# Attention of a six-stage decoder block on one core: row-tiled scores, column-tiled values, reciprocals folded into the turning matmuls

## The reference

```python
q, k, v = (x @ Wq.T), (x @ Wk.T), (x @ Wv.T)        # each (8, 256, 16, 32)
scores = einsum('bqhd,bkhd->bhqk', q, k) / sqrt(32)
scores = where(causal_mask, scores, finfo.min)
attn = einsum('bhqk,bkhd->bqhd', softmax(scores), v)
x = layernorm(x + attn.reshape(8, 256, 512) @ Wo.T)
```

## Time and profile before

| | us |
|---|---|
| median of 3 runs | 3803.29 |
| the profiled execution's own time | 3801.35 |
| its span | 3799.4 |
| attention, first matmul to last addition | 23.1 to 529.4 |
| layer norm after it begins | 531.1 |

### The profile page before, as it was taken

One profiled execution on the slowest core, in us unless ns is written; L12 is line 12 of the kernel. 1 busy time (PEld: TensorE's weight loads), 2 busy tenths in 40 slices (PEclk: granted clock), 3 DMA queues, 4 the chain that ended last, 5 costly groups with the idle time before them and its releaser, 6 DMA issues. The chain is left out here.

```text
span 3799.4 us, 82582 instructions
## 1 busy us (share of the span) xinstructions
PE 3343.9 (88%) x29419; PEld 2405.9 (63%) x29438; DVE 2678.5 (70%) x4880; ACT 2129.4 (56%) x5227; POOL 1348.2 (35%) x1657
## 2 busy tenths in 40 slices
PE   7999978724799999999999999999999999994285
PEld 6788855523567677677776676767776767672142
DVE  3445449977477777777777777777777777776896
ACT  2233330023577777777776767767777677763453
POOL 0000014401345454545454454545454545440000
PEclk9999989967899999999999999999999999996698
DMA  2000011100110101001101010001010100001201
GB/s 106 13 7 12 12 74 41 36 19 19 42 35 20 33 18 41 30 24 29 41 18 36 18 40 29 24 30 40 18 35 19 41 29 24 29 18 45 89 1 45
DMA packets 44277, 121.73 MB, mean 32 GB/s; under 512 B 5856, under 2 KB 11104, under 8 KB 40544
## 3 DMA queue, kind: packets, MB, share of 16 engines
q1 hardware_dynamic: 43872, 116.35, 9.5%
HBM read 111.80 MB, written 4.54 MB: 31 GB/s over the span
## 5 line engine op out<-in xcount | busy, mean ns | idle before, releaser
L1885 DVE TENSOR_TENSOR delta_Pb<-delta_bank,delta_lev 128x512 f16<-128x512 f32 x448 | 311.9, 696 | 228.4 <-PE delta_bank L2198 228.4
L1877 DVE SCALAR_TENSOR_TENSOR delta_F<-delta_bank,delta_cw,delta_F 128x510 f32<-128x510 f32 (+1 forms) x512 | 381.8, 746 | 94.1 <-ACT delta_far L1695 82.6
L1491 POOL TENSOR_TENSOR delta_F<-delta_F,delta_far 128x506 f32<-128x506 f32 x256 | 282.6, 1104 | 435.7 <-DVE delta_F L1877 434.8
L2172 PE MATMUL delta_bank<-delta_xh,delta_qkvh 128*128 128x512 f16 x1024 | 389.8, 381 | 5.4 <-DVE delta_qkvl L1845 3.0
L2172 PE MATMUL delta_bank<-delta_xl,delta_qkvh 128*128 128x512 f16 x1024 | 390.1, 381 | 0.0
L2172 PE MATMUL delta_bank<-delta_xh,delta_qkvl 128*128 128x512 f16 x1024 | 389.6, 380 | 0.0
L1689 ACT ACTIVATE delta_F<-delta_bank,delta_cw 128x512 f32<-128x512 f32 x256 | 178.3, 697 | 313.4 <-PE delta_bank L2172 312.2
L1894 DVE CAST delta_XT<-delta_bank 128x512 f16<-128x512 f32 x448 | 309.5, 691 | 45.5 <-PE delta_bank L2221 45.3
L1471 POOL TENSOR_SCALAR_AFFINE_SELECT delta_LA<-delta_LA 128x512 f32<-128x512 f32 x128 | 81.3, 635 | 651.6 <-DVE delta_LA L1905 649.9
L2157 PE MATMUL delta_bank<-delta_zh,delta_xh 128*128 128x256 f16 x1024 | 280.2, 274 | 0.6 <-ACT delta_gz L1717 0.6
L2157 PE MATMUL delta_bank<-delta_zl,delta_xh 128*128 128x256 f16 x1024 | 279.9, 273 | 0.0
(11 more groups left out here) (311 smaller groups left out, 9776.9 us busy)
## 6 DMA issues: line engine op xcount, KB each, us to landing
delta_Gb<-g_rows SPq DMA_DIRECT2D x66, 512.0 KB, 5.2
delta_st_qkv<-in_Wqkv SPq DMA_DIRECT2D x17, 1024.0 KB, 8.2
conv_T<-filters SPq DMA_DIRECT2D x32, 256.0 KB, 3.1
delta_st_zo<-in_Wz SPq DMA_DIRECT2D x16, 512.0 KB, 8.4
delta_st_zo<-in_Wout SPq DMA_DIRECT2D x16, 512.0 KB, 6.2
ffn_ahead_W<-in_W SPq DMA_DIRECT2D x2, 4096.0 KB, 17.2
conv_ahead_C<-in_ctx_rev SPq DMA_DIRECT2D x1, 6144.0 KB, 17.3
attn_xt<-in_xT SPq DMA_DIRECT2D x10, 512.0 KB, 4.0
```

What stands on the lines that cost most here:

```text
L1491: gp.tensor_tensor(dst[:, :, 3:256], dst[:, :, 3:256], src[:, :, 0:253], ALU.add)\
L1877: ve.scalar_tensor_tensor(dst, src, cw_tap(i, 3 - lag), dst, ALU.mult, ALU.add)\
L1885: ve.tensor_tensor(left(Pb[:, lvl, :, :], lvl), comp(bank[5], lvl), bc(lev[:, lvl, :].rearrange("p (n s) -> p n s", s=1 << lvl), 1, 8), AL ...
L2172: ins = te.matmul(bk[:, :], ww[:, QKV[job], kc, :], xx[:, kc, tok:tok + 512], start=(m == 0), stop=(m == 11))
```

## The change

The hardware loop is gone: `attn_uses` writes out the order, for `GROUPS` = 32 jobs. A job is one batch's four heads that share a 128-feature tile, both query halves together.

- q is no longer padded. It is copied like k, by ScalarE, in one instruction of 128 partitions (`Q2`). A head's scores are a matmul on its own 32 partitions (`Q[32 * r:32 * r + 32, ...]`), with r = 0 to 3 in four banks of `sc4`. The mask comes first: one bf16 matmul of 384 columns a head, then 256 columns of scores for the second queries, then 128 for the first. `sc4` has one copy: the scores of job j wait for the exponentials of job j-1.
- `transposes` become `turn`: each 128x128 block of exponentials is the stationary operand of an ordinary float32 matmul with `dg`, a diagonal matrix of the reciprocal row sums. GpSimd makes the eight diagonals of a job in one instruction of 1024 elements a partition. `normalise` and the transposes L300 go.
- `values` has v's 32 columns as stationary operand and the turned probabilities as moving one (256 columns, then 128), and writes partitions 32r to 32r+31 of `vb`: the output is made transposed, as the Wo product needs it; ScalarE copies it (`acopy`).
- All projections and Wo products share one bank, `ub`. Up to three of these uses stand in each slot of a job: the first ahead of the turns, the second ahead of the third turn, the third ahead of the values.
- Each weight matrix has its own semaphore; q0, k0, v0, v1 of batch 0 come first. Eight batches are projected, none for nothing. The second slice of x is loaded ahead of X.

```diff
-        Qz2 = sb("Qz", [P, 2, NH, S])
...
+        Q2, K2 = sb("Q", [P, 2, KC, S]), sb("K", [P, 2, KC, S])
...
+                for r in range(4):
+                    te.matmul(sc4[:, r, 0:3 * P], ib[:, :], mneg[:, :, :].rearrange("p a n -> p (a n)"),
+                              start=True, stop=False)
+                for r in range(4):
+                    te.matmul(sc4[:, r, P:3 * P], Q[32 * r:32 * r + 32, P:2 * P], K[32 * r:32 * r + 32, 0:2 * P],
+                              start=False, stop=False)
+                for r in range(4):
+                    last = te.matmul(sc4[:, r, 0:P], Q[32 * r:32 * r + 32, 0:P], K[32 * r:32 * r + 32, 0:P],
+                                     start=False, stop=True)
...
+                    last = te.matmul(bk[:, i * P:(i + 1) * P], pr[:, j % 2, r, block_ * P:(block_ + 1) * P],
+                                     dg[:, q, r, :], start=True, stop=True)
...
+                for r in range(4):
+                    h = 4 * kc + r
+                    te.matmul(vb[32 * r:32 * r + 32, 0:S], V[:, 0, h * HD:(h + 1) * HD],
+                              PT[:, r // 2, (r % 2) * S:(r % 2 + 1) * S], start=True, stop=False)
+                for r in range(4):
+                    h = 4 * kc + r
+                    last = te.matmul(vb[32 * r:32 * r + 32, P:S], V[:, 1, h * HD:(h + 1) * HD],
+                                     PT[:, 2, r * P:(r + 1) * P], start=False, stop=True)
...
+            for s in range(GROUPS + 2):
+                if s < GROUPS:
+                    scores(s)
+                count = len(slots[s])
+                if count > 0:
+                    use(at)
+                if 1 <= s <= GROUPS:
+                    turn(s - 1, 0)
+                    turn(s - 1, 1)
+                if count > 1:
+                    use(at + 1)
+                if 1 <= s <= GROUPS:
+                    turn(s - 1, 2)
+                if count > 2:
+                    use(at + 2)
+                if 1 <= s <= GROUPS:
+                    values(s - 1)
+                at += count
...
+            for j in range(GROUPS):
+                pool.wait_ge(rec.sem, rec.at(j + 1))
+                if j:
+                    pool.wait_ge(tr.sem, tr.at(3 * j))
+                gp.tensor_tensor(dg[:, :, :, :].rearrange("p q h n -> p (q h) n"), bc(ident[:, :], 1, 8),
+                                 bc(ri[:, :, :].rearrange("p q h -> p (q h)"), 2, P), ALU.mult)\
+                    .then_inc(dgs.sem, 1)
...
+            def exps(j):
+                act.wait_ge(nms.sem, nms.at(j + 1))
+                if j >= 2:
+                    act.wait_ge(tr.sem, tr.at(3 * (j - 1)))
+                for r in range(4):
+                    se.activation(pr[:, j % 2, r, P:3 * P], sc4[:, r, P:3 * P], ACT.Exp, bias=nm[:, j % 2, 1, r:r + 1],
+                                  scale=SC, accum_out=rs[:, j % 2, 1, r:r + 1])
+                    last = se.activation(pr[:, j % 2, r, 0:P], sc4[:, r, 0:P], ACT.Exp,
+                                         bias=nm[:, j % 2, 0, r:r + 1], scale=SC,
+                                         accum_out=rs[:, j % 2, 0, r:r + 1])
+                last.then_inc(ex.sem, 1)
...
+            for s in range(GROUPS + 2):
+                uses = slots[s]
+                if 1 <= s <= GROUPS:
+                    reciprocals(s - 1)
+                if s < GROUPS:
+                    maxima(s)
+                if uses and uses[0][1] == "w0":
+                    added(uses[0][0], 0)
+                if 1 <= s <= GROUPS:
+                    ptcopy(s - 1, 0)
+                    ptcopy(s - 1, 1)
+                if len(uses) > 1 and uses[1][1] == "w1":
+                    added(uses[1][0], 1)
+                if 1 <= s <= GROUPS:
+                    ptcopy(s - 1, 2)
```

More of the change, by code:

```diff
@@ L189, with attn_uses @@
 NH, HD = 16, 32
-BEHIND = {0: ["p0"], 1: ["t1", "p1"], 2: ["w1"], 3: ["p2"], 4: ["p3"], 5: ["p4"], 6: ["p5"], 7: ["p6"],
-          8: ["t0", "p7"], 10: ["w0"], 11: ["p8"], 12: ["p9"]}
-USES = [name for slot in sorted(BEHIND) for name in BEHIND[slot]]
+GROUPS = B * KC
+def attn_uses():
+    ahead = ["q0", "k0", "v0", "v1", "q1", "k1", "q2", "k2", "q3", "k3"]
+    queue = [(n, name) for n in range(B) for name in ahead]
+    first, queue = queue[:4], queue[4:]
+    slots = []
+    for s in range(GROUPS + 2):
+        uses = [(s // KC - 1, name) for name in ("w0", "w1")] if s % KC == 1 and s > 1 else []
+        take = 3 - len(uses)
+        slots.append(uses + queue[:take])
+        queue = queue[take:]
+    return first, slots
 def attn_stage(nc, X, consts, x_dram, xT, WqT, WkT, WvT, WoT):
@@ L200, in attn_stage @@
         sb, counter = pt.sb, pt.counter
-        bank = pt.banks()
+        sc4 = ctx.enter_context(nc.psum_tensor("attn_scores", [P, 4, 512], F32))
+        tb = [ctx.enter_context(nc.psum_tensor(f"attn_turned{i}", [P, 512], F32)) for i in range(2)]
+        vb = ctx.enter_context(nc.psum_tensor("attn_values", [P, 512], F32))
+        ub = ctx.enter_context(nc.psum_tensor("attn_proj", [P, 512], F32))
         ident = consts["ident"]
@@ new lines, in bank_free, with use @@
+            def bank_free(i):
+                if i == 0:
+                    return
+                n, name = order[i - 1]
+                if name[0] == "w":
+                    pe.wait_ge(add.sem, add.at(2 * n + int(name[1]) + 1))
+                else:
+                    pe.wait_ge(pc.sem, pc.at(number[n, name] + 1))
+            def use(i):
+                n, name = order[i]
+                c = int(name[1])
+                bank_free(i)
+                if name[0] == "w":
+                    if n == 0 and c == 0:
+                        pe.wait_ge(wl["o"].sem, wl["o"].at(1))
+                    pe.wait_ge(atc.sem, atc.at(KC * (n + 1)))
+                    for kc in range(KC):
+                        last = te.matmul(ub[:, :], aT[:, kc, c * P:(c + 1) * P], W["o"][:, kc, :],
+                                         start=(kc == 0), stop=(kc == KC - 1))
+                    last.then_inc(wo.sem, 1)
+                    return
+                if name == "q0":
+                    pe.wait_ge(load[n % 2].sem, load[n % 2].at(n // 2 + 1))
+                if n == 0 and c == 0:
+                    pe.wait_ge(wl[name[0]].sem, wl[name[0]].at(1))
@@ L275, in project @@
[L275 to L309, removed]
@@ L312, in _ @@
[L312 to L321, removed]
@@ new lines, in use @@
+                last.then_inc(proj.sem, 1)
+            for i in range(4):
+                use(i)
+            pe.wait_ge(cst.sem, cst.at(4))
+            at = 4
+            for s in range(GROUPS + 2):
[16 more added lines that the diff above has]
+                at += count
@@ new lines, in acopy @@
+            def acopy(j):
+                act.wait_ge(av.sem, av.at(j + 1))
+                se.activation(aT[:, j % KC, :], vb[:, 0:S], ACT.Copy).then_inc(atc.sem, 1)
+            for i in range(4):
+                take(i)
+            at = 4
+            for s in range(GROUPS + 2):
+                count = len(slots[s])
+                if count > 0:
+                    take(at)
+                if s < GROUPS:
+                    exps(s)
+                if count > 1:
+                    take(at + 1)
+                if count > 2:
+                    take(at + 2)
+                if 1 <= s <= GROUPS:
+                    acopy(s - 1)
+                at += count
@@ L534 @@
+            dve.wait_ge(add.sem, add.at(2 * B))
 CH, HR = 32, 8
```

323 lines of the change are left out of this document (99 added, 224 removed).

## The result

The kernel after takes 3697.47 us in the median (3694.0 to 3700.08, 4 runs) against 3802.94 of the kernel before in the same sessions: a ratio of 0.972, 95% interval 0.9706 to 0.9735, 105 us less. The forecast was 3766 with a range from 3700, so the direction is right and the size is far off; the time is that of the rival in which all tiles work at once, 3703.

What follows compares the result with a forecast made beforehand. TensorE's stream was taken to bound attention: 14.31 us a job, times 32 is 458, with start, 6 us of bank waits and 9 idle ending attention at 492 against 529.4, 37 less: 3766 us, range 3700 to 3812.

Steps and rivals of the forecast that it cites:

- the rival in which all tiles work at once: Attention jobs: scores and values at 0.66 us each, 12.3 a job, total 3703 us; chance 0.20.
- Which engine sets the end: Attention stage: TensorE's stream sets the end; other engines' long idle entries are waits for it or steps it covers.
- Scores and values: Four-head products on different tiles: partial overlap, five half-times rather than eight, 1.65 us each instead of 2.64.
- Changes of tile: Four switches of tile shape in each job, 0.17 us each, 0.68 together; bounds 0 and 0.72.
- Masks: Four bf16 matmuls of 384 columns a job in place of eight of 128: 0.64 us, the low end.
- Turns: Twelve float32 products of 128 columns a job in place of twelve transposes: 2.64 us against 1.2, a loss.
- Projections and Wo: TensorE's projection and Wo products, unchanged at 28.2 us a batch, 7.05 a job.
- Ninth batch: Projecting eight batches rather than nine takes 21.1 us off TensorE's stream, already in the sum.
- Start: First projections begin at 15.7 us instead of 23.1; jobs begin at 29.9 with 10.6 us of work done.
- Gaps: TensorE idle time: 6 us waiting for bank `ub` in some 24 slots, 9 us at the end.
- Diagonals: GpSimd's diagonal instruction taken as 2.5 us; the rival has it at 5, delaying turns, 3790 us; chance 0.11.
- The single score copy: One copy of `sc4`: next scores' wait for the exponentials is hidden by 5 us of turns, uses and values.

Runs made afterwards that it cites:

- by_head: Kernel after with each head's two products standing together, for scores and for values, instead of four and four; 3700.62 us, ratio 0.9722.
- one_row_tile: Kernel after with all four heads' score products using row tile 0, the first 32 partitions of q and k; 3776.47 us, ratio 0.9919.
- split_values: Kernel after with a job's first four value products ahead of the third turn, adding two changes of tile a job; 3708.8 us, ratio 0.9748.
- ninth: Kernel after with the projections of a ninth batch put back at the end of the queue; 3706.96 us, ratio 0.9739.
- one_col_tile: Kernel after with all four heads' value products writing column tile 0, partitions 0 to 31 of the values bank; 3757.58 us, ratio 0.9875.
- scaled_dve: Kernel after with GpSimd scaling the exponentials in place, transposes as turns, and VectorE copying the second projection; 3671.5 us, ratio 0.9649.

## Why the prediction was wrong, step by step

*Which engine sets the end*: right. TensorE is busy for 472.5 of 480 us before and for 330 of 330 in the middle of the kernel after, and no other engine appears in front of it for long.

*Scores and values*: this is the step that failed. The term "four products then take five half-times rather than eight", 1.65 each, measured 0.86 and 0.79 with a change of tile inside. The two records of a float32 product do share a tile, but a tile that waits does not hold up the rest (by_head), so four products need two half-times. With masks and changes, the job's four terms were 4.62 and measured 0.75 + 0.86 + 0.79 = 2.40. That difference of 2.2 in 32 jobs is 71 us, of which projections and turns give back 4; the forecast missed by 68.5. One tile at a time costs 1.95 and 1.93 more in a middle job, so the overlap is full, 4 x (0.44 + 0.22) = 2.64 falling to 0.66 plus changes: the rival at 12.3 a job, against 12.22 measured.

*The two rules of the Trainium skill*: the first group of scores, 4 x 0.44 = 1.76 one after another (1.83 in one_row_tile), takes 0.53, a factor of 3.3 to 3.5. The Trainium skill ("TensorE: Matmul & The Clock Gate", Measured speedup vs the span model) gives 3.07 for four row tiles with 512 moving columns; the trace has 256 columns and somewhat more than that, and no run here has 512. Full overlap was weighed too lightly against a mechanism that I had only argued. The Trainium skill ("TensorEngine Tiling (Array Packing)", Key Properties) says that a change of tiling mode drains the engine. A change does cost time here, 0.14; that draining is what takes it, no run shows.

*Changes of tile*: 0.17 put, 0.14 measured by split_values; 4 us too dear over the stage. *Masks*: 0.64, right (0.75 with the change behind them). *Turns*: 2.64, right (1.79 + 0.89). *Projections and Wo*: 7.05, right (12.22 - 2.40 - 2.68 = 7.14).

*Ninth batch*: 21.1 us of work in the sum; taking it away was worth 13, because without it the last slots are partly idle and partly at the lower clock. *Start*: first matmul at 15.89, jobs from 30.96 rather than 29.9; waiting for all weights costs 7.9. *Gaps*: 15 us put. The last addition ends near 425.4, and 30.96 + 32 x 12.22 - 10.6 = 411.4, which leaves 14. That the sum agrees is luck, for the parts were wrong: the 6 us for the one bank are next to nothing inside the middle slots, about 2 us are idle up to 80 us, and more than the 9 fall at the end, about 1.5 of them by the lower clock that no term had.

*Diagonals*: put at 2.5, measured 1.90, and doubling them cost only 3.6 us. That rival is dead. *The single score copy*: hidden, as put; no mask of the kernel after waits for the exponentials.

## What to carry to other kernels

Float32 products on four different 32-row or 32-column tiles ran together here in little more than the time of one (0.53 and 0.45 against 0.44), in both orders tried; pay the change of tile (0.14 us) once for a group of them. Work that only TensorE can do is what to save there: turning with a diagonal costs twice a transpose, while an idle GpSimd can scale beforehand. When TensorE's stream gets shorter, a copy queued behind a long group on another engine becomes the next limit, and moving it is worth nothing before and about 20 us after. A slot can stand at such a limit without a wait in the trace: compare the time from copy to use with TensorE's own, before pricing what a shorter stream will bring.

## What the runs showed of the hardware that was not expected

- The granted clock fell to 0.50 behind a stretch in which TensorE was busy all the time, but with one row tile of four (one_row_tile, 2.8 us); four tiles at once (0.86 us of scores) and one column tile of four (2.7 us of values) kept it at 1.00. It fell in 8 of 19 jobs.
- It also fell to 0.50 for about 3 us in the last turns of the kernel after, behind waits of TensorE (2.17 us the longest); in ninth and one_col_tile, where these waits are filled, the same turns keep their pace.
- GpSimd's product of two broadcast operands, 1024 elements a partition, took 1.90 us, where two of 512 in the delta rule take 2 x 1.27; in place on 512 elements (scaled_dve) it took 1.05.
